# GpSimd waits for every second gathered group to land before it issues the next one

## The reference

```python
for l in range(n_layers):                       # 2 layers
    W = einsum('rb,bio->rio', coeffs[l], bases[l])   # 8 relations
    h = einsum('ni,rio->rno', x, W)                  # every node under every relation
    msg = h[edge_type, src] * deg_inv[dst][:, None]  # one row of 256 for each edge
    agg = segment_sum(msg, dst, num_segments=num_nodes)
    x_new = agg + x @ self_loops[l]                  # relu after the first layer
```

## Time and profile before

| what | us |
|---|---|
| median of three executions | 2587.59 |
| the profiled execution, first to last instruction (its span) | 3411.3 |
| of it: up to the first gather | 356.7 |
| gathers of layer 0, first issue to last | 356.7 to 1706.8 |
| last gather of layer 0 to first of layer 1 | 76.5 |
| gathers of layer 1, first issue to last | 1783.3 to 3089.8 |
| after the last gather | 321.5 |

### The profile page before, as it was taken

The page is one execution under the profiler, slowest core; times in us unless marked ns, Lnnn a source line. Parts: engine busy times, 40 slices in busy tenths (PEclk is TensorE's granted clock), DMA queues, the critical chain, the costliest instruction groups (busy, mean ns, idle before and its releaser), DMA issues. The chain is left out here.

```text
span 3411.3 us, 37691 instructions
## 1 busy us (share of the span) xinstructions
PE 2398.6 (70%) x9525; PEld 1737.8 (51%) x9528; DVE 1074.1 (31%) x3125; ACT 626.8 (18%) x1391; POOL 1649.4 (48%) x1712
## 2 busy tenths in 40 slices
PE   6999357777777777776882766666666666566287
PEld 3788235555555555554561544444444444455065
DVE  3787022222222222222220333333233333234233
ACT  4455101111111111110120011111111211110033
POOL 0000655555555555555506555555655555551645
PEclk9999678888888888888895877777777777788587
DMA  8764433334333333433423332333332223231531
GB/s 225 250 232 192 139 100 123 128 125 133 123 124 124 126 124 125 128 122 112 131 90 93 88 91 87 88 87 88 91 88 84 86 87 90 85 87 32 164 110 54
DMA packets 159887, 397.24 MB, mean 116 GB/s; under 512 B 34926, under 2 KB 92241, under 8 KB 145932
## 3 DMA queue, kind: packets, MB, share of 16 engines
q0 software_dynamic: 81648, 219.65, 22.1%
q10 hardware_dynamic: 35772, 124.12, 9.4%
q1 hardware_dynamic: 42337, 51.93, 5.5%
HBM read 260.70 MB, written 138.94 MB: 117 GB/s over the span
## 5 line engine op out<-in xcount | busy, mean ns | idle before, releaser
L515 POOL DMA_INDIRECT gnn_ring<-table,g_idx x1564 | 1512.7, 967 | 1418.2 <-PE gnn_pagg L558 680.0
L558 PE MATMUL gnn_pagg<-gnn_ring,gnn_oh 128*128 x3904 | 1215.4, 460 | 483.7 <-issue 427.0
L558 PEld LDWEIGHTS gnn_pagg<-gnn_ring,gnn_oh 128*128 128x128 f32 x3904 | 838.0, 228 | 886.9 <-issue 759.7
L542 DVE TENSOR_TENSOR gnn_oh<-gnn_col,g_dst 128x256 f32<-128x256 f32 x976 | 408.9, 426 | 1471.2 <-DVEq L49 1214.0
L800 ACT COPY second_wr<-gnn_pm 128x512 f32<-128x512 f32 x196 | 103.0, 597 | 1107.8 <-DMA pre_bs<-in_L_gnn_bases 992.7
L1054 ACT ACTIVATE gnn_qe<-gnn_pq,gnn_bq 128x128 f32<-128x128 f32 x98 | 36.1, 368 | 1078.0 <-remote 1036.1
L402 PE MATMUL pre_psum<-pre_whigh,pre_high 128*128 128x512 f32 x392 | 159.0, 406 | 13.1 <-DVE pre_low L309 8.1
L336 DVE SCALAR_TENSOR_TENSOR second_wr<-pre_bs,pre_cr,second_wr 128x512 f32<-128x512 f32 x232 | 159.5, 748 | 2.8
L744 PE MATMUL gnn_pm<-gnn_whigh,gnn_high 128*128 128x512 f32 x392 | 157.5, 402 | 3.5 <-issue 2.5
L744 PE MATMUL gnn_pm<-gnn_whigh,gnn_low 128*128 128x512 f32 x392 | 153.8, 392 | 6.8 <-issue 6.7
L744 PE MATMUL gnn_pm<-gnn_wlow,gnn_high 128*128 128x512 f32 x392 | 152.9, 390 | 4.2 <-issue 4.2
(11 more groups left out here) (174 smaller groups left out, 2382.6 us busy)
## 6 DMA issues: line engine op xcount, KB each, us to landing
table<-pre_rows ACTq DMA_DIRECT2D x49, 1024.0 KB
table<-second_wr ACTq DMA_DIRECT2D x48, 1024.0 KB
gnn_ring<-table,g_idx POOLq DMA_INDIRECT x1564
bucket<-gnn_zrow SPq DMA_DIRECT2D x16, 650.0 KB
g_xT<-bucket SPq DMA_DIRECT2D x20, 520.0 KB, 6.3
pre_bs<-in_L_gnn_bases SPq DMA_DIRECT2D x32, 240.0 KB
pre_bs<-in_L_gnn_bases SPq DMA_DIRECT2D x30, 256.0 KB
x1T<-gnn_x1T ACTq DMA_DIRECT2D x49, 128.0 KB
```

Source lines behind the costliest of these rows:

```text
L515: eng.indirect_dma_start(self.ring[:, q % RG, t, 0:D], None, self.g.table[self.l][:, :], bass.IndirectOffsetOnAxis(ap=self.g.idx[:, at:at ...
L542: self.nc.vector.tensor_tensor(self.oh[:, h, :, :], self.col[:, :].unsqueeze(1).to_broadcast([P, n, P]), self.g.dst[:, ds(q * TPG + h * n, ...
L558: mm = nc.tensor.matmul(pagg[:, k, 0:self.width], self.oh[:, h, i, :], self.ring[:, ds(q & (RG - 1), 1), t, 0:self.width].rearrange("p o n ...
```

## The change

After the last gather of every odd group, POOL waits until that group's slot semaphore has the group's total, the very condition that SP waits for in `count`. The total is moved to a function of its own, `landings`. Number and order of the gathers, the ring and all other waits stay. There are 98 such waits in each layer.

```diff
+BURST = 2
...
+    def landings(self, q):
+
+        return 16 * sum(min(TPG, NT - p * TPG) for p in range(q % RG, q + 1, RG))
+
     def count(self, eng, between=None):
 
         for q in range(NG):
-            eng.wait_ge(self.landed[q % RG], 16 * sum(min(TPG, NT - p * TPG) for p in range(q % RG, q + 1, RG)))
+            eng.wait_ge(self.landed[q % RG], self.landings(q))
...
                eng.indirect_dma_start(self.ring[:, q % RG, t, 0:D], None, self.g.table[self.l][:, :],
                                        bass.IndirectOffsetOnAxis(ap=self.g.idx[:, at:at + 1], axis=0)
                                        ).then_inc(self.landed[q % RG], 16)
+            if q % BURST == BURST - 1:
+                eng.wait_ge(self.landed[q % RG], self.landings(q))
```

## The result

The changed kernel takes 3174.06 us (median of 3162.09 to 3183.22) against 2587.49 before: 1.227 times as long (95% interval 1.224 to 1.230), 587 us more. The forecast was 3130 us in a range of 2900 to 3250.

What follows compares the result with a forecast made beforehand. The prediction took POOL, issuing gathers without a pause, as the bound of timed executions. 196 waits at 2.85 us less 16 us gave 543 us; 2588 + 543 = 3131, stated as 3130 us, range 2900 to 3250 us.

Steps and rivals of the forecast that it cites:

- POOL as the bound: In timed executions POOL issues gathers without a pause, one every 1.23 us, 19.7 us for a block's 16 gathers.
- the profiled span should grow by 0 to 150 us: Changed kernel's profiled span against 3411.3 us: little growth, since POOL's new block stays under what PE takes there.
- 666 us outside: Time outside the gathers: 356.7 us ahead of them, 25 between the layers and 284 behind.
- The gap (b): POOL's queue behind each wait: 3.15 us between two gathers, 0.30 already there, so 2.85 us more at each wait.
- The last term: From L512 to the next gather's start where POOL has been idle: 0.73 us read, 0.75 us taken.
- Cover (d): Added waits beside PE's work: POOL's block grows from 19.7 to 25.4 us, above PE's; zero hidden, bound 64 us.
- Not slower (3): Rival: POOL's slack hides the wait and PE stays the bound, 2588 us; chance 0.04 including no effect at all.
- POOL's 39 us too long: Sum with POOL as the bound of the kernel before: 2627 us, 39 us (1.5%) above the timed 2587.6.
- PE's 216 us too short: Sum with PE as the bound of the kernel before: 2372 us, 216 us below the timed 2587.6.
- Less clock (4): Rival: more holes in PE's work lower its clock, making layer 0 blocks slower; 3260 us and up, chance 0.07.
- Eights of 9.7 us: Sign in the changed kernel's profile: POOL's gathers come in eights, each eight 9.7 us long.
- POOL's waits for PE under 250 us: Sign in the changed kernel's profile: POOL's waits for PE fall from 680 us to under 250.

Runs made afterwards that it cites:

- The two cuts: Kernel before without the fourth gather of each group from group 16 on: 2337.4 us; kernel before with 8 of 24 L744 matmuls per layer 0 block: 2580.9 us.
- three_gathers: Kernel before without the fourth gather of each group from group 16 on, PE's work the same: 2337.4 us, ratio 0.904.

## Why the prediction was right or wrong

**POOL as the bound: right, for a reason that was partly wrong.** I inferred from the earlier trace rows and the median that a timed execution has POOL without a pause. The two cuts showed it. But I took the 824 us for something that the profiled execution has alone. It is most likely the chip: on one kind of chip timed and profiled executions agree (2586.8 and 2585.1 us), and on another kind timed ones take 3377 us, near the 3411. Whether the profile of 3411.3 us came from such a chip is not on record. The step "the profiled span should grow by 0 to 150 us" failed, it fell by 241; it seems to have compared two kinds of chips.

**The pace and the rest.** 1.23 us a gather was taken, 1.266 measured; 666 us outside was taken, 605 measured, of it 220 behind the last gather in place of 284. The pace was worked out from the 666, so the two errors offset each other, and neither reaches the forecast, which adds to the measured 2588.

**The gap (b): right.** 1.8 us for the landing (1.85), 0.6 for the load chain (0.56), 0.75 to the gather (0.75): 3.15 us in all, and the median gap is 3.13 in layer 1 and 3.22 in layer 0. The last term was rightly read but wrongly named. As a price of any restart it made the forecast of one wait per group 87 us too long. It also makes the waits without a load behind them 1.1 us cheaper and not 0.6; and these are seven in a layer, not eight, since group 16 has a load already. That is 6 us in all.

**The missing term.** 543 us were forecast, 587 measured. All of the 44 us lie in layer 0: half the forecast is 272 us, layer 1 has 270 and layer 0 317. 32 of them are landings and loads delayed by the 1 MB stores; the other 12 are not explained. I had taken 1.8 us for every landing. The profile that I read gives no other figure, 1.91 us on average over layer 0's groups, but the one of 2585.1 us does, 2.41 us there and 1.93 in layer 1: the size of the term was to be had only from a profile of the kind of chip that was timed. The wait of 5.0 us in the earlier trace rows is no sign of it. It is SP's wait for the first group, from 358.4 us on, and takes in the issue of four gathers.

**Cover (d): right.** At 19.3 us a block (the median in three_gathers, where PE bounds layer 0) PE lies under POOL's 20.2 before and 26.7 after; nothing was hidden. Half the waits gave half the cost.

**The rivals.** Not slower (3): false where the kernel before takes 2588 us. Its condition, that POOL has slack because PE is held up, is what the profile of 3411.3 us shows, and on a chip with such times the outcome was even on the other side. I gave that world no chance of its own, although the profile that I read looks like it; that the timed executions were of the other kind was inferred from two sums, POOL's 39 us too long and PE's 216 us too short. Less clock (4): the granted clock fell from 0.98 to 0.89 in layer 0 and from 0.89 to 0.82 in layer 1, and POOL's pace covered it. The Trainium skill (DMA: Bandwidth & Descriptors, section "Anatomy of one DMA — SWDGE (gpsimd) path") gives 2.0 us and bytes / 436e3 for one such transfer, an estimated 2.3 us for 128 KB. Measured are 1.85 us from the end of the issue and 2.8 from its start, so the estimate lies between the two, and in the prediction it was set against the first alone.

**What the profile was to show.** Eights of 9.7 us, gaps of 3.0 to 3.3 us, the load behind the wait: seen. Gaps released by a DMA: 14 are so labelled, the other 180 PE or issue. POOL's waits for PE under 250 us: 351, by that same label.

## What to carry to other kernels

A wait for a transfer that was issued just before costs its whole landing time and also everything behind it in the queue that used to run ahead; a wait for a transfer issued four gathers (5 us) earlier, at the same place, cost next to nothing (3 us for 196 of them). If such a wait is needed, put it last, directly ahead of the instruction that needs it. And when a profile's span and the timed median differ by a third, find out first whether the two come from the same kind of chip: an engine that waits in the one can be the bound in the other, and the sign of a change can differ between them. A label of an idle time names the last wait passed, not the longest; where instructions of the queue stand in the gap, their starts tell more.

## What the runs showed of the hardware

An indirect DMA of 128 rows of 1 KB takes 0.95 us of GpSimd and 0.30 us to the next one, 1.25 to 1.29 us in all, whether the landings are waited for every four gathers, every eight, every sixteen or not at all, and on every chip seen. Its data is confirmed 1.85 us after the end of its issue by the median, and up to 4.6 us after it in the layer with the stores of 1 MB. The same stores stretch a load of one number from SBUF from 0.29 us to as much as 0.96. A gather that carries the wait itself starts 0.24 us after the landing; behind a separate instruction that carries it the gather starts 0.75 us after that one. And two of the chips seen run the kernel before 1.3 times as long as the others.
